# Dense stage of a two-layer transformer kernel: key-value sums held in PSUM for a whole batch, with TensorE and VectorE written out

## The reference, cut to what matters

```
x  = layernorm(x)
q, k, v = x @ w_qkv.T                       # 16 heads of 16
k  = elu(k) + 1
kv = einsum('bnhd,bnhm->bhdm', k, v)        # one sum over the 2048 tokens of a batch
z  = 1 / (einsum('bnhd,bhd->bnh', q, k.sum(axis=1)) + 1e-6)
...
shared expert: h = silu(x @ Ws1.T + bs1) * (x @ Ws3.T + bs3), with its time coordinate
               out = [time, h] @ Ws2.T + bs2
```

## Time and profile before

| what | value |
|---|---|
| median of 3 runs | 1988.62 us (1985.88 to 1989.11) |
| time of the profiled execution | 1988.8 us |
| its span, first to last instruction | 1987.0 us |
| PE busy over the span | 1414.6 us (71%) |
| DVE busy | 1508.0 us (76%) |
| ACT busy | 1192.5 us (60%) |
| POOL busy | 1084.9 us (55%) |
| mean granted TensorE clock | 0.880 of full speed |

### The profile page before, as it was taken

One profiled execution on the slowest core, in us unless ns is written; L12 is line 12 of the kernel. 1 busy time (PEld: TensorE's weight loads), 2 busy tenths in 40 slices (PEclk: granted clock), 3 DMA queues, 4 the chain that ended last, 5 costly groups with the idle time before them and its releaser, 6 DMA issues. The chain is left out here.

```text
span 1987.0 us, 64075 instructions
## 1 busy us (share of the span) xinstructions
PE 1414.6 (71%) x22151; PEld 978.0 (49%) x22152; DVE 1508.0 (76%) x3763; ACT 1192.5 (60%) x2964; POOL 1084.9 (55%) x1088
## 2 busy tenths in 40 slices
PE   3469999698896544555400079999997789999755
PEld 3435555465554433444300046666665456666544
DVE  7876777565664788778689879999996668888745
ACT  8647787556665466788656434444443567777643
POOL 6667777533333876678546612222222567777643
PEclk9999999899998677778655589999998999999878
DMA  8547666689994334334459833333332112222137
GB/s 253 180 130 182 186 193 177 171 186 203 216 219 135 109 116 145 115 117 140 126 140 196 161 71 66 65 63 61 65 65 51 46 44 53 53 53 53 44 108 231
DMA packets 453363, 247.78 MB, mean 125 GB/s; under 512 B 323517, under 2 KB 440832, under 8 KB 452736
## 3 DMA queue, kind: packets, MB, share of 16 engines
q1 hardware_dynamic: 440674, 210.71, 42.9%
q0 software_dynamic: 12576, 35.67, 5.9%
HBM read 79.52 MB, written 73.44 MB: 77 GB/s over the span
## 5 line engine op out<-in xcount | busy, mean ns | idle before, releaser
L197 PE MATMUL ps<-all_late,l_xq_T 128*128 128x352 f16 x1536 | 244.4, 317 | 173.3 <-DVEq L185 162.7
L197 PEld LDWEIGHTS ps<-all_late,l_xq_T 128*128 (+1 forms) x1536 | 147.9, 99 | 265.2 <-DVEq L185 163.1
L469 POOL TENSOR_TENSOR ffn_h<-ffn_fq_val,ffn_h 128x704 f16<-128x704 f32 x64 | 97.4, 1522 | 286.7 <-ACT ffn_h L464 286.7
L197 PE MATMUL ps<-l0moe_W,all_xT_all 128*128 128x16 f16 (+2 forms) x1152 | 190.3, 312 | 38.7 <-ACT all_xT_all L828 22.3
L647 ACT ACTIVATE ffn_th<-ps 128x352 f32<-128x352 f32 x128 | 59.3, 463 | 178.8 <-PE ps L197 178.8
L1362 POOL TENSOR_TENSOR all_late<-experts_se,all_mhalf 128x4 f32<-128x4 f32 (+1 forms) x77 | 76.3, 992 | 160.6 <-DVE experts_se L1471 148.7
L2211 POOL TENSOR_TENSOR all_late<-ret_pm,all_late 128x512 f16<-128x512 f32 x128 | 145.4, 1157 | 19.3 <-ACT all_late L2117 19.3
L197 PEld LDWEIGHTS ps<-l0moe_W,all_xT_all 128*128 (+1 forms) x1152 | 83.9, 100 | 120.6 <-ACT all_xT_all L828 26.0
L632 PE MATMUL ps<-all_late,ffn_hT 128*128 128x256 f16 x1088 | 131.7, 276 | 8.0 <-ACT l_xq_T L657 4.4
L1628 PE MATMUL ps<-all_ident,both_o 128*128 128x128 f16 x256 | 26.4, 265 | 148.5 <-ACT both_oT L1726 134.4
L197 PE MATMUL ps<-moe_E,experts_gT 128*128 x864 | 117.6, 276 | 16.5 <-DMA experts_gT<-slots_dram 12.0
(11 more groups left out here) (299 smaller groups left out, 4663.6 us busy)
## 6 DMA issues: line engine op xcount, KB each, us to landing
rows_dram<-all_late SPq DMA_DIRECT2D x72, 256.0 KB
ret_v<-ret_vpad SPq DMA_DIRECT2D x256, 64.0 KB
front_xin<-x SPq DMA_DIRECT2D x16, 512.0 KB, 4.4
x_dram<-front_x SPq DMA_DIRECT2D x16, 512.0 KB, 5.3
all_late<-x_dram SPq DMA_DIRECT2D x64, 128.0 KB
z_dram<-all_late SPq DMA_DIRECT2D x64, 128.0 KB
both_zin<-z_dram SPq DMA_DIRECT2D x16, 512.0 KB
both_xin<-x SPq DMA_DIRECT2D x16, 512.0 KB
```

Source lines behind the costliest of these rows:

```text
L197: mm = pe.matmul(out, lhs[a], rhs[b], start=first and n == 0, stop=last and n == 2, skip_group_check=True)
L469: eng.tensor_tensor(lo, self.shaped(t, hi), hi, ALU.subtract).then_inc(self.lo, 1)
```

## The change

`sums` becomes two PSUM banks, 4 and 5. A batch's 16 tiles are summed in one of them, and the next batch takes the other. VectorE copies the finished sum to `kv_sum` once per batch, in place of an add per four tiles, so `kv_sum` need not be set to zero first. TensorE's product waits only at the first tile of batches 2 and 3, for the copy two batches back. TensorE's and VectorE's programs are written out; ScalarE's stays a loop. `unrolled` gets a parameter that gives a tile its number modulo 4, as `pipeline` does.

```diff
-def unrolled(count, stages):
+def unrolled(count, stages, slots=LAG):
...
-                stage(Tile(s - skew, (s - skew) % LAG, (s - skew) // LAG))
+                stage(Tile(s - skew, (s - skew) % LAG, (s - skew) // LAG, (s - skew) % slots))
...
-        sums = ps[:, 4, 0:C * (P + 2)].rearrange("p (c m) -> p c m", c=C)
+        sums = [ps[:, 4 + u, 0:C * (P + 2)].rearrange("p (c m) -> p c m", c=C) for u in range(2)]
...
-                if t.slot4 == 0:
-                    pe.wait_ge(s_kvadd, t.n // 4 + 1)
+                batch, first = t.n // TB, t.n % TB == 0
+                if first and batch >= 2:
+                    pe.wait_ge(s_kvadd, batch - 1)
...
-                        ins = pe.matmul(sums[:, c, 0:P + 1], keys[x], vals[y], start=c == 0 and n == 0 and t.slot4 == 0,
+                        ins = pe.matmul(sums[batch % 2][:, c, 0:P + 1], keys[x], vals[y], start=c == 0 and n == 0 and first,
...
-            pipeline(pe, TILES, [(7, down), (3, kv_product), (0, project)], 4)
+            unrolled(TILES, [(7, down), (3, kv_product), (0, project)], 4)
...
-            dve.sem_inc(s_kvadd, 1)
...
-            dve.memset(kv_sum[:], 0.0).then_inc(s_fill, 1)
-            dve.wait_ge(s_fill, 3)
+            dve.wait_ge(s_fill, 2)
...
-                if t.slot4 != 3:
-                    return
-                dve.wait_ge(s_kvs, done(t))
-                dve.wait_ge(s_kvadd, t.n // 4 + 1)
-                acc = kv_sum[:, bass.ds(t.n // TB, 1)].rearrange("p o c m -> p (o c) m")
-                dve.tensor_tensor(acc[:, :, 0:P + 1], sums[:, :, 0:P + 1], acc[:, :, 0:P + 1], ALU.add).then_inc(s_kvadd, 1)
+                if t.n % TB == TB - 1:
+                    dve.wait_ge(s_kvs, done(t))
+                    dve.tensor_copy(kv_sum[:, t.n // TB, :, 0:P + 1], sums[t.n // TB % 2][:, :, 0:P + 1]).then_inc(s_kvadd, 1)
...
-            pipeline(dve, TILES, [(4, add_sums),
+            unrolled(TILES, [(4, add_sums),
```

## The result

The changed kernel takes 1990.80 us in the median of 20 runs, against 1986.76 us of the kernel before, 20 runs on the same chip: ratio 1.0022, 95% interval 1.0012 to 1.0032. It is slower by 0.2%, where 0.5% faster was predicted; the range of 1975.0 to 1984.6 us does not hold it. One of the changed kernel's 20 runs took 4540 us and is left out of the ratio; the other 19 have a median of 1990.26 us. The profiled execution took 1995.83 us (span 1994.0).

The account below looks back on a forecast made before the run. TensorE was taken to bound the dense stage; -10.9 (wait), -0.2 (step 7), +0.5 (new waits) and +0.6 (tail) made -10.0 us, from 1988.62 to 1978.6 us, with an 8-in-10 range of 1975.0 to 1984.6 us.

Parts of the forecast that it names:

- What bounds the kernel: Dense stage: TensorE, busy 221.52 of 230.00 us, bounds it, and only its waits can be won.
- The wait in the product, -10.9 us: Product L1131, steps 7 to 63: waits for VectorE's add in 14 steps, 0.78 us each, vanish.
- What could hold TensorE instead: Dense stage: keys' low part has some 2 us to spare; GpSimd's slow recovery brings 0.5 us of new waits.
- Nothing for the loop: Dense stage: TensorE's loop is covered by queued matmuls, VectorE's by waits for ScalarE; removal saves nothing.
- Adds and memset: VectorE, dense stage: twelve of 16 adds vanish, copies cost the add's 0.42 us, the dropped memset gains 0.
- The tail, +0.6: Stage's end after the last projection: ScalarE can't follow the full gain, so 0.6 us is given back.
- The signs: Profile marks, dense stage: 56 steps in some 219 us, GpSimd's idle before L1270 under 10 us, marks for rivals.
- GpSimd as the bound: Dense stage: GpSimd limits the gain to about 3 to 5 us, giving 1984.6 us; chance 0.10.
- Nothing is left: Another equal wait replaces the product's, or a later stage loses the gain: 1988.6 us; chance 0.08.
- The code arrives late: TensorE's written-out code: about 11 more block loads at 3.8 us each cost 42 us, giving 2019 us; chance 0.04.
- Slower: Whole kernel: the outcome of a slower median, beyond 0.2%; chance 0.04.

Follow-up runs that it names:

- e1: The changed kernel with the expert load ahead of the row gather (`rows_in`) in SyncE's step; 1975.88 us, ratio 0.9948 to the kernel before.
- e3: The kernel before, loops, sums and adds kept, with only the expert load moved ahead of `rows_in` on SyncE; 1975.40 us, ratio 0.9951.
- e4: The kernel before with TensorE's and VectorE's dense-stage programs written out, sums and adds kept; 1990.63 us, ratio 1.0029.
- e7: The kernel before with VectorE's program alone written out; ratio 1.0015 to the kernel before.
- e13: e4 with `expert_lo` moved behind `hidden_lo` in VectorE's step, all work kept; 1991.31 us, ratio 1.0024 to the kernel before.
- e9: The changed kernel again, unedited, for a second set of runs and a second profile; 1987.76 us, ratio 1.0020 to the kernel before.
- e12: e4 with `expert_lo` taken out of the steps, one memset ahead of the stage setting the low parts to zero; 1998.81 us, ratio 1.0050 to the kernel before.
- e10: e4 with VectorE's `expert_lo` replaced by a memset, leaving out the low part of the experts' weights; 1994.51 us, ratio 1.0037 to the kernel before.
- e8: The changed kernel with the expert load one place later on SyncE, behind the store of z; 1999.81 us, ratio 1.0079 to the kernel before.
- e6: The kernel before with TensorE's program alone written out; ratio 1.0033 to the kernel before.

## Why the prediction was wrong

*What bounds the kernel.* It said that TensorE bounds the stage and that its waits can be won. The second half is right in size (e1 and e3 win 10 us) and wrong in place: beside TensorE's 15.65 us per four steps stood a ring of 16.31.

*The wait in the product, -10.9 us.* The surplus was measured rightly. The failed step is the next one, **"What could hold TensorE instead"**. It took 2.0 us of spare time of the low part of the keys from one place, step 19. That spare time was the add's own delay: VectorE and ScalarE had the keys ready, and TensorE was late. It then asked what each *engine* could do, and put 0.5 us on GpSimd's recovery. It never asked what would hold ScalarE once TensorE no longer did. ScalarE's waits change places: before 27.2 us for TensorE (19.2 for the product, 8.0 for the projection) and 5.2 us for the expert load, after the change none and 34.8 us. The row of that load was in the waits of the kernel before, 5.2 us in 5 times, and the last load with its 1.64 us was even read the earlier trace rows, but only as part of the tail.

*Nothing for the loop.* That TensorE's loop costs it no time was right where TensorE sets the pace: e1 (written out) and e3 (looped) both take 219.1 us. So the 108 ns per compare-and-branch that the prediction quoted from the Trainium skill (Advanced Engine Details and Errata, section Control Flow Timing) stay covered. That its removal costs nothing was wrong where the ring does: e4 is slower by 0.29%. By what path is open: the order on VectorE against GpSimd's scatters shifts, and the longest waits can cost more than themselves through the clock (below), but e7 and e13 speak against the first as the whole cause, and the steps hold only part of the loss.

*Adds and memset.* Right: 4 copies of 0.42 us.

*The tail, +0.6.* It took 20.2 us from the last L1119 to the experts' stage, before 18.9: 1.3 us, and 1.2 in e9. Same sign, twice the size.

*The signs.* Of the two named for "GpSimd as the bound" one came: ScalarE waits for L1269 ahead of L1179 (17.1 us, before 2.5). The other, GpSimd's steps without idle time, did not: it is idle for 19.1 us before L1266 (before 17.2), where my own forecast had named under 10. The rival is half right. GpSimd's two steps are 7.8 of the ring's 16.4 us, but it has gaps of up to 2.7 us; it is a link and no bound, and in e1 it keeps 3.91 us per step.

*The rivals.* "Nothing is left" is what came, with the cause it named first, another wait of the same length in the product's place; I gave it 0.08 since the bank has no second reader, which is an argument on the bank and says nothing of a ring. "The code arrives late" fell: 12 blocks, no gap with them. (Its count of 11 came partly by luck: of the 14 steps that it called written out only the first 12 are, and 2 of the 3 blocks had come by their end.) "Slower" had 0.04, all of it for late code; a loss from the written-out programs by a shift of phase was not thought of.

## What to carry to other kernels

When an engine waits in every n-th step, follow the wait back from queue to queue, the DMA queue's too, and see whether the chain closes on itself, before pricing the wait; the length of the closed chain is then the pace, whatever engine is busiest, and the releaser that the trace names is only the last to arrive. Ask of each wait that would vanish who was hidden behind it: an engine's wait for one thing can hide its wait for another. In a program that issues DMAs in order, such as SyncE's here, a load that others need soon should not stand behind one that waits for a landing: here one line's order was worth 0.5%, and a second staging buffer, with the load three steps earlier, 0.7%.

## What the hardware showed that I had not expected

**A GpSimd scatter's length depends on what VectorE started just before.** A scatter of `moe_pos_hi` takes 0.96 us alone, and up to 1.72 us where `expert_lo` of 0.94 us is already under way at its start: it then ends 0.83 us behind `expert_lo`'s end (0.85 + 0.83 = 1.68 us in most turns of e4). The same holds for a shorter operation with two SBUF inputs: in e12 the hidden row's low part (L1232, 0.42 us) ends 0.32 us into a scatter that takes 1.16. Where `expert_lo` starts after the scatter, by 0.01 us or more, the scatter takes 0.96 to 1.22 us. With a float16 memset in its place the mean is 1.85 us, with the operation behind it (e10).

**A stall of some 2 us can cost TensorE its clock.** In e4, at the turn of the ring near the end of the stage:

```profile
355.55 0.50 PE L1131 MATMUL ps<-dense_v,dense_k 128*128 128x129 f16 x6 [1.95 <-DVE l0moe_kv_sum L1239]
355.89 4.43 PE L197 MATMUL ps<-l0moe_W,all_xT_all 128*128 128x512 f16 x12
```

```profile
356.20:357.60 1.40, 1.40 (x5) 0.48 (x4) 1.40 (x6) 1.40 (x5) 1.25 (x3) 0.50 0.60 126
```

After 1.95 us of idle time the granted clock is 0.50, the 1.2 GHz level, and the twelve matmuls take 4.43 us where they take 2.75 elsewhere: 1.7 us more. The same came in e10 after a stall of 2.25 us and in e12 after 2.35. In e8 it came twice, each time after two stalls close together, 1.52 and 0.72 us and later 1.14 and 0.72. The first of them, PE in order of time:

```profile
174.77 0.52 PE L1132 MATMUL ps<-dense_v,dense_k 128*128 128x129 f16 x6 [1.52 <-DVE dense_k L1226]
176.01 4.45 PE L197 MATMUL ps<-l0moe_W,all_xT_all 128*128 128x512 f16 x12 [0.72 <-DVE dense_kmax L1210]
```

Stalls of 1.92 us (e10), 1.91 us (e13) and 1.84 us (e6), and 1.09 and 0.72 us close together in the changed kernel, passed without it, so the length of the stall alone does not decide. Up to step 55 the surplus of e4 is 7.9 us and that of the kernel before 7.6; in the last two turns, with this event, it is 3.8 us against 1.8. So the 2.3 us by which e4's surplus exceeds that of the kernel before lie nearly all there, and the other 11 turns of the ring are the same (16.30 us on average against 16.27). In the changed kernel no single stall in these steps is over 1.1 us, and its clock stays at 1.00.
